# A two-layer graph network on one core: node steps at the end of a pass taken in pairs, one-hot matrices as stationary operands, splits in PSUM, and a preparation that no longer waits for its loads

## The chip, the cores and the metric

One core of a Trainium2 chip runs one launch. The time is device microseconds from start to end of the launch; smaller is better. TensorE is called PE below (its weight loads PEld), VectorE DVE, ScalarE ACT, GpSimd POOL and SyncE SP, as the profile does.

## The reference

A graph of 12,500 nodes with 96 features and 412,500 directed edges, sorted by their target `dst`. Three rounds over all edges have to be computed, each needing the nodes' result of the round before:

```python
e = relu(edge_weight1 @ W_l0 + b_l0) @ W_l1 + b_l1
for layer in (0, 1):                      # two GINE convolutions
    msg = relu(x[src] + e)
    h = x + segment_sum(msg, dst)
    x = relu(relu(h @ Wi0 + bi0) @ Wi1 + bi1)
x = layernorm(x_in + x)
edge_feat = mlp_bn(edge_attr_4)           # linear, relu, batch norm over the edges
m = mlp_bn(concat(x[row], x[col], edge_feat))
x = layernorm(x + segment_sum(m, col) + mlp_bn(x))
```

`mlp_bn` is a linear layer, relu and a normalization with mean and variance over all rows.

## The kernel before

The program is a preparation block (`setup`), three edge passes made by one function `edge_pass` (named `conv0`, `conv1` and `last`), and `finish`. Each is a block of its own: its end is a barrier of all engines.

**An edge pass.** The padded edges are cut into S = 124 slabs of T = 26 tiles of 128 edges. V = 4 slabs make an iteration, so a pass has 31 iterations. A slab is worked on in 7 chunks of four tiles (the last has two). For each tile POOL issues one indirect DMA (`gather`, L254) that fetches the 128 source rows `x[src]` into `got[j]`; there are four such buffers, so POOL can run up to four slabs ahead of the add that consumes them. That is 3,224 gathers in a pass and 9,672 in all. GROUPS cuts the 26 gathers of a slab into two sets with a semaphore each, chunks 0 to 3 and chunks 4 to 6.

For each chunk q a software pipeline (`staged`) runs these steps, each engine in program order: PE `hidden` (L509, the first edge layer), ACT `relu_hidden` (L522), PE `pre` (L1034, the second edge layer in f32, into `ps_pre`), DVE `add_rows` (L598, adds the gathered rows in PSUM), ACT `relu_message` (L543, the message as bf16 part 0), DVE `subtract_first` (L550), ACT `second_part` (L557, bf16 part 1), DVE `third_part` (L563, bf16 part 2), DVE `one_hot` (L1095, for each edge a row of 112 entries with a one at its target's place in the slab's window of 112 nodes), and PE `segment`, whose matmuls `sum_window` (L569) sum the edges by target: for each tile three matmuls, one for each bf16 part, with the 128 x 96 part stationary and the 128 x 112 one-hot moving. At the slab's end DVE `add_window` (L1090) adds the 96 x 112 window from PSUM to `sums`, which holds features by nodes. In `last` there are also squares and sums for the batch norm.

**Node steps.** Once the windows have passed 256 nodes, a node step applies the two node layers (and in `conv1` the layer norm and the products for the last pass), stores its rows to DRAM and lets the next begin. 46 of the 50 steps of `conv0` and of `conv1` are interleaved with the windows; the last four run after the windows, one after the other in a loop (`node_steps`). In `conv0` a step is PE L738, ACT L780, PE L743, ACT L788 twice, PE L748, DVE L822, a store by ACT (L727). In `conv1` it is PE L738, ACT L780, PE L754, DVE L828 to L836, ACT L797, DVE L841 to L847, PE L761, ACT L803, PE L767, ACT L807, PE L774, DVE L855 to L863, and three stores. The next pass gathers from the stored rows, so its first gather comes after the last step's stores, the block's end and a reload of four index tiles by SP (L251).

**Preparation.** `setup` lets POOL issue the gathers of the first two slabs (52) while DVE turns the targets into window positions `rel` and `near_b` and counts whether every edge lies in its window (`fits`). SP issues 25 loads, waits for all 20 constants among them (L323, one of them 4.8 MB of node columns into `sums`), and only then stores `near_b` (L326), waits for it and ends. At the start of `conv0` DVE splits the edge weights `w_f` (128 x 3224 f32, in SBUF) into three bf16 parts (`split`, L273 and L276), which are stored and read back in rows by every slab; it also sets two rows of `sums` (L637, L639). In each of the 31 iterations of `conv0` it splits a piece of the edge attributes in the same way (`split_piece`, L991 and L995, 128 x 416).

## Time and profile before

| | us |
|---|---|
| median of three runs (lowest, highest) | 12338.1 (12335.53, 12362.99) |
| the profiled execution, its own time | 12336.89 |
| its span, first to last instruction | 12335.1 |
| busy: PE, DVE, ACT, POOL | 9812.2, 7390.6, 4942.9, 9165.5 |
| first gather of `conv0`'s block, of `conv1`, of `last` | 94.89, 4116.98, 8223.39 |
| last gather begins | 12252.23 |

The busy times are how long each engine executed something; register, branch and DMA-issuing instructions of the other queues are not in them, but POOL's gathers are. Idle time is put down to what ended it; "issue" is time in which an engine waited for nothing that the profile shows. The rows used here are in the section after the change.

### The profile page before, as it was taken

How to read it: one execution, taken by the hardware profiler on the slowest of the kernel's cores; microseconds unless marked ns; L12 is line 12 of the kernel's file. 1: busy time of each engine (PE TensorE's matmuls, PEld its weight loads, DVE VectorE, ACT ScalarE, POOL GpSimd, SP SyncE). 2: the span in 40 equal slices, each digit the busy share in tenths (PEclk: the TensorE clock that was granted, in tenths of full speed). 3: DMA queues.
4: the chain of work that ended last, by engine and by line, in shares of the span. 5: the costliest groups of instructions: out<-in, count | busy, mean ns of one | idle time of the engine just before them, and what ended most of it. 6: DMA issues, size and time to landing. Idle time of an engine off the chain costs nothing. (4 is left out here: it accounts for less than half of the span.)

```text
span 12335.1 us, 196060 instructions
## 1 busy us (share of the span) xinstructions
PE 9812.2 (80%) x53154; PEld 7907.9 (64%) x53154; DVE 7390.6 (60%) x15235; ACT 4942.9 (40%) x11027; POOL 9165.5 (74%) x9676
## 2 busy tenths in 40 slices
PE   5877777777777788899999999977777777777777
PEld 4766666666666566677777777756666666666666
DVE  5544444444444455566666666657777777777777
ACT  2333333333333344444444444434444444444444
POOL 7777777777777677777777777757777777777775
PEclk9999999999999655555555555555555555555555
DMA  3222222222222222222222222222222222222222
GB/s 92 46 48 47 48 48 47 49 47 47 49 47 47 61 51 50 52 55 56 55 56 54 56 55 56 54 45 52 51 54 52 53 52 53 52 53 52 53 52 53
DMA packets 580897, 647.13 MB, mean 52 GB/s; under 512 B 411337, under 2 KB 411818, under 8 KB 579851
## 3 DMA queue, kind: packets, MB, share of 16 engines
q0 software_dynamic: 309504, 476.02, 18.4%
q1 hardware_dynamic: 216086, 143.43, 5.0%
q10 hardware_dynamic: 54896, 23.80, 0.7%
q14 instruction: 346, 2.83, 0.1%
q8 instruction: 65, 1.06, 0.0%
HBM read 604.68 MB, written 39.43 MB: 52 GB/s over the span
## 5 line engine op out<-in xcount | busy, mean ns | idle before, releaser
L1034 PE MATMUL ps_pre<-w_e,conv_hid 97*128 97x96 f32 x12896 | 3283.8, 435 | 1200.0 <-DVE conv_part L563 1188.3
L1034 PEld LDWEIGHTS ps_pre<-w_e,conv_hid 97*128 97x128 f32 x12896 | 2877.5, 327 | 1925.9 <-issue 1597.7
L1034 PE MATMUL ps_pre<-last_w_q,last_hid 128*128 128x96 f32 x6448 | 1626.0, 432 | 1056.9 <-issue 700.4
L1034 PEld LDWEIGHTS ps_pre<-last_w_q,last_hid 128*128 128x128 f32 x6448 | 1440.2, 327 | 1446.5 <-issue 1022.9
L543 ACT ACTIVATE conv_part<-ps_pre 128x384 bf16<-128x384 f32 x1736 | 815.8, 470 | 3482.4 <-DVE ps_pre L598 3478.0
L569 PE MATMUL ps_win<-conv_hot,conv_part 128*96 128x112 bf16 x19344 | 2164.8, 301 | 0.6 <-DVE conv_part L563 0.6
L569 PEld LDWEIGHTS ps_win<-conv_hot,conv_part 128*96 128x96 bf16 x19344 | 2106.0, 203 | 1.1 <-DVE conv_part L563 0.9
L254 POOL DMA_INDIRECT early_got<-p_rows,early_idx x1612 | 1523.6, 945 | 570.3 <-issue 491.0
L254 POOL DMA_INDIRECT early_got<-h_rows,early_idx x1612 | 1523.0, 945 | 537.5 <-issue 489.1
L254 POOL DMA_INDIRECT early_got<-in_x_rows,early_idx x1612 | 1541.8, 956 | 493.3 <-issue 490.7
L254 POOL DMA_INDIRECT conv_got<-in_x_rows,early_idx x1612 | 1531.3, 950 | 503.6 <-issue 503.3
L254 POOL DMA_INDIRECT last_got<-p_rows,early_idx x1612 | 1523.8, 945 | 491.4 <-issue 491.4
L254 POOL DMA_INDIRECT conv_got<-h_rows,early_idx x1612 | 1521.9, 944 | 491.4 <-issue 490.8
L598 DVE TENSOR_TENSOR ps_pre<-ps_pre,early_got 128x384 f32<-128x384 f32 x1302 | 698.1, 536 | 1685.0 <-PE ps_pre L1034 701.2
L522 ACT ACTIVATE conv_hid<-ps_hid 96x512 f32<-96x512 f32 x1736 | 973.5, 561 | 1027.9 <-PE ps_hid L509 957.3
L598 DVE TENSOR_TENSOR ps_pre<-ps_pre,conv_got 128x384 f32<-128x384 f32 x868 | 464.9, 536 | 1397.2 <-PE ps_pre L1034 576.6
L509 PE MATMUL ps_hid<-conv_row,w_hid 12*96 12x512 bf16 x1736 | 1088.0, 627 | 128.5 <-issue 98.7
L1095 DVE TENSOR_TENSOR conv_hot<-ps_own,rel 128x448 bf16<-128x448 f32 x1736 | 1019.5, 587 | 238.6 <-PE ps_win L569 216.2
L569 PE MATMUL ps_win<-last_hot,last_part 128*97 128x112 bf16 x9672 | 1083.2, 301 | 0.3 <-DVE last_part L563 0.3
L569 PEld LDWEIGHTS ps_win<-last_hot,last_part 128*97 128x97 bf16 x9672 | 1056.7, 207 | 0.6 <-DVE last_part L563 0.4
L563 DVE TENSOR_TENSOR conv_part<-ps_pre,conv_part 128x384 bf16<-128x384 f32 x1736 | 905.4, 522 | 100.7 <-issue 84.2
L557 ACT CAST conv_part<-ps_pre 128x384 bf16<-128x384 f32 x1736 | 786.8, 453 | 414.7 <-DVE ps_pre L550 394.1
(183 smaller groups left out, 10053.1 us busy)
## 6 DMA issues: line engine op xcount, KB each, us to landing
conv_row<-ea_parts SPq DMA_DIRECT2D x372, 84.5 KB
last_row<-ea_parts SPq DMA_DIRECT2D x372, 84.5 KB
early_got<-in_x_rows,early_idx POOLq DMA_INDIRECT x1612, 2.5
conv_got<-in_x_rows,early_idx POOLq DMA_INDIRECT x1612, 2.5
early_got<-h_rows,early_idx POOLq DMA_INDIRECT x1612, 2.5
conv_got<-h_rows,early_idx POOLq DMA_INDIRECT x1612
early_got<-p_rows,early_idx POOLq DMA_INDIRECT x1612
last_got<-p_rows,early_idx POOLq DMA_INDIRECT x1612
```

The source lines that it names most:

```text
L254: gp.indirect_dma_start(to[:, t * C:(t + 1) * C], None, table, bass.IndirectOffsetOnAxis(index[:, t:t + 1], 0)).then_inc(sem, 16)
L509: pe.matmul(ps["hid"][0][0:HC, 0:nt * P], w_hid[:], row[r][AT:AT + K, t0 * P:(t0 + nt) * P], start=True, stop=True).then_inc(s["hid"], 1)
L522: act.activation(hid[b][0:C, 0:nt * P], ps["hid"][0][0:C, 0:nt * P], ACT.Relu).then_inc(s["rhid"], 1)
L543: act.activation(tiles_of(part0[q % NC_], nt, C1), m3, ACT.Relu).then_inc(s["part0"], 1)
L557: act.copy(tiles_of(part1[b], nt, C1), tiles_of(ps["pre"][b], nt, C)).then_inc(s["part1"], 1)
L563: v.tensor_tensor(tiles_of(part2[b], nt, C1), tiles_of(ps["pre"][b], nt, C), tiles_of(part1[b], nt, C1), ALU.subtract).then_inc(s["part2"], 1)
L569: mm = pe.matmul(bank[0:M, 0:width], part[:, t * C1:t * C1 + M], hot_b[:, t * width:(t + 1) * width], start=start and i == 0, stop=stop an ...
L598: v.tensor_tensor(at, at, got[j][:, t0 * C:(t0 + nt) * C], ALU.add).then_inc(s["add"], 1)
L1034: mm = pe.matmul(ps["pre"][q % 2][:, t * C:(t + 1) * C], hid[q % 2][0:P if last else C1, t * P:(t + 1) * P], w_q[j % U][:, c * C:(c + 1) * ...
L1095: v.tensor_tensor(hot[q % 2][:, 0:nt * W].rearrange("p (t w) -> p t w", w=W), iota[:, 0:W].unsqueeze(1).to_broadcast([P, nt, W]), rel[:, b ...
```

## The change

Besides new code for the ends of two passes it consists of six edits.

1. **Pairs at the end.** The four last node steps of `conv0` and `conv1` are no longer a loop. `end_steps` takes 512 nodes at a time (`w` = 0, 1) and writes the stages of both out in turn, with buffers for each in the idle gather buffers and a second PSUM bank. Stores are issued by SP, the last one also without the padding row, whose own store (`none`) is issued first. In `conv1` POOL clears the 1,024 last columns of `sums`.
2. **One-hots as weights.** `sum_tile` makes one matmul for each tile: the one-hot (128 x 112) is stationary, the three parts side by side (128 x 288, or 291 in `last`) move. The window is now 112 nodes by three parts of 96; at the slab's end DVE adds the three (`fold_window`), PE turns the result (`turn_window`), and DVE adds it to `sums` from there. The parts have NB = 4 buffers of all three instead of seven and two and two.
3. **Splits in PSUM.** ACT copies the weights into seven PSUM banks and makes the bf16 parts; DVE subtracts in PSUM. `copy_piece` does the copy for the attributes.
4. **Counts by one operand.** `rel` is shifted by a PSUM operand instead of an SBUF copy of it, and each of the two counts of edges inside is two single-operand comparisons that also sum.
5. **Loads.** The preparation no longer waits for the constants; `conv0` does, before its first matmul. The 4.8 MB of node columns are issued by ACT once the targets have landed. The two rows of `sums` are set at the preparation's end.
6. **Groups.** The gathers of a slab are in three sets: chunks 0 to 3, 4 and 5, and 6.

The core of the diff (the end steps are given as their `conv0` half; that of `conv1` has the same form):

```diff
-GROUPS = [(0, (NC_ + 1) // 2 - 1), ((NC_ + 1) // 2, NC_ - 1)]
+GROUPS = [(0, (NC_ + 1) // 2 - 1), ((NC_ + 1) // 2, NC_ - 2), (NC_ - 1, NC_ - 1)]
...
-                     (gb_msg, a["gb_msg"]), (w_wide, a["w_wide"]), (sums[0:C, :], a["x_cols"]),
+                     (gb_msg, a["gb_msg"]), (w_wide, a["w_wide"]),
...
-                sp.wait_ge(s["const"], 16 * len(loads))
                 sp.wait_ge(s["near"], 32)
...
+                act.wait_ge(s["dst"], 16)
+                act.wait_ge(s["near"], 16)
+                act.dma_start(sums[0:C, :], a["x_cols"]).then_inc(early["cols"], 16)
...
-                go(v.tensor_tensor(rel3, rel3, base_all[:].unsqueeze(2).to_broadcast([P, S, T]), ALU.subtract))
+                go(v.tensor_tensor(rel3, rel3, ps["base"][0][:, 0:S].unsqueeze(2).to_broadcast([P, S, T]), ALU.subtract))
...
-                go(v.tensor_scalar(seen, rel[:], 0.0, None, ALU.is_ge))
-                done()
-                go(v.scalar_tensor_tensor(out=seen, in0=rel[:], scalar=float(W), in1=seen,
-                                          op0=ALU.is_lt, op1=ALU.mult, accum_out=tmp[:, 0:1]))
+                def count(at, x, bound):
+                    go(v.tensor_scalar(inside[0:x.shape[0], 0:x.shape[1]], x, bound, 0.0, ALU.is_ge, ALU.add,
+                                       accum_out=tmp[0:x.shape[0], at:at + 1]))
+                    done()
+                count(10, rel[:], 0.0)
+                count(11, rel[:], float(W))
...
+                count(12, near_f[:], 0.0)
+                count(13, near_f[:], float(R))
...
+                go(v.memset(sums[C:C + 2, :], 1.0))
+                done()
+                go(v.memset(sums[C:C1, :], 0.0))
...
+                def sum_tile(pe, bank, hot_b, q, t, start, stop):
+                    parts = part[q % NB][:].rearrange("p (i x) -> p i x", i=3)[:, :, t * C1:t * C1 + M]
+                    return pe.matmul(bank[0:W, 0:3 * M].rearrange("p (i c) -> p i c", i=3), hot_b[:, t * W:(t + 1) * W], parts,
+                                     start=start, stop=stop)
...
-                        split(go, done, v, w_f[:], [x[:] for x in w_p])
+                        for i in range(2):
+                            for c, (bank, at) in enumerate(cuts):
+                                v.wait_ge(s["wx"], c + 1)
+                                v.wait_ge(s[f"wp{i}"], c + 1)
+                                v.tensor_tensor(bank, bank, w_p[i][:, at], ALU.subtract).then_inc(s[f"wrest{i}"], 1)
...
+                        for w in ENDS:
+                            pe.wait_ge(s["e_z"], w + 1)
+                            pe.matmul(one[w][0:C, :], w_conv[l][1][0:C, :], z_end[w][0:C], start=True, stop=True).then_inc(s["e_b"], 1)
+                        for w in ENDS:
+                            pe.wait_ge(s["e_cols"], w + 1)
+                            for t in range(TW):
+                                mm = pe.transpose(ps["pre"][w][:, t * C:(t + 1) * C], z_end[w][0:C, t * P:(t + 1) * P], ident[0:C, 0:C])
+                            mm.then_inc(s["e_turn"], 1)
...
+                def copy_piece(act, k):
+                    act.wait_ge(s["ef"], 16 * (k + 1))
+                    need(act, s["estep"], k)
+                    act.copy(ps["e"][0][:, 0:D * PIECE], e_f[:]).then_inc(s["ecopy"], 1)
...
+                    def turn_window(k, q):
+                        j, c, _, _ = chunk(q)
+                        if c == NC_ - 1:
+                            pe.wait_ge(s["wsum"], k * V + j + 1)
+                            pe.transpose(turned[j % U][0:M, :], folded[:, 0:M], ident[0:W, 0:W]).then_inc(s["turned"], 1)
...
-                    staged(pe, ITERS, Q, [(0, hidden_rows), (1, pre), (3, segment)],
+                    staged(pe, ITERS, Q, [(0, hidden_rows), (1, pre), (4, turn_window), (3, segment)],
...
+                    def fold_window(k, q):
+                        j, c, _, _ = chunk(q)
+                        if c == NC_ - 1:
+                            bank = ps["win"][j % U]
+                            v.wait_ge(s["seg"], Q * k + q + 1)
+                            need(v, s["turned"], k * V + j)
+                            v.tensor_reduce(folded[:, 0:M], bank[0:W, 0:3 * M].rearrange("p (i c) -> p c i", i=3), AX_X,
+                                            ALU.add).then_inc(s["wsum"], 1)
...
-                    plan += [(1, add_rows)]
+                    plan += [(1, add_rows), (4, add_window)]
...
-                        node_steps(eng, (ITERS - START) * PAIRS, [(s[f"win{r}"], ITERS * PAIRS) for r in range(U)])
+                        end_steps(eng)
```

## Rows read from the trace of the kernel before

**Rows 1.** The page's first part: busy time, share and count of each engine.

```profile
PE 9812.2 (80%) x53154; PEld 7907.9 (64%) x53154; DVE 7390.6 (60%) x15235; ACT 4942.9 (40%) x11027; POOL 9165.5 (74%) x9676
```

**Rows 2.** Groups of POOL: the gathers of the first two passes, by buffer.

```profile
L254 POOL DMA_INDIRECT early_got<-in_x_rows,early_idx x1612 | 1541.8, 956 | 493.3 <-issue 490.7 <-DMA early_idx<-in_src_t 2.3 <-DVE ps_pre L598 0.3
L254 POOL DMA_INDIRECT conv_got<-in_x_rows,early_idx x1612 | 1531.3, 950 | 503.6 <-issue 503.3 <-DVE ps_pre L598 0.3
...
L254 POOL DMA_INDIRECT early_got<-h_rows,early_idx x1612 | 1523.0, 945 | 537.5 <-issue 489.1 <-DMA early_idx<-in_src_t 46.6 <-DVE ps_pre L598 1.8
L254 POOL DMA_INDIRECT conv_got<-h_rows,early_idx x1612 | 1521.9, 944 | 491.4 <-issue 490.8 <-DVE ps_pre L598 0.6
```

**Rows 3.** POOL's timeline: start, duration, instruction, idle time before it.

```profile
18.64 5.13 POOL L254 DMA_INDIRECT early_got<-in_x_rows,early_idx  x1 [0.30 <-issue]
24.08 3.95 POOL L254 DMA_INDIRECT early_got<-in_x_rows,early_idx  x1 [0.30 <-issue]
...
44.12 3.23 POOL L254 DMA_INDIRECT early_got<-in_x_rows,early_idx  x1 [0.30 <-issue]
...
94.89 0.94 POOL L254 DMA_INDIRECT conv_got<-in_x_rows,early_idx  x1 [12.60 <-issue]
...
102.69 4.42 POOL L254 DMA_INDIRECT conv_got<-in_x_rows,early_idx  x1 [0.30 <-issue]
...
4116.98 0.94 POOL L254 DMA_INDIRECT early_got<-h_rows,early_idx  x1 [46.61 <-DMA early_idx<-in_src_t]
...
8223.39 0.94 POOL L254 DMA_INDIRECT early_got<-p_rows,early_idx  x1 [79.27 <-DMA early_idx<-in_src_t]
...
12252.23 0.95 POOL L254 DMA_INDIRECT last_got<-p_rows,early_idx  x1 [0.31 <-issue]
```

**Rows 4.** DVE's timeline in the preparation and at the start of `conv0`.

```profile
18.26 3.52 DVE L371 TENSOR_TENSOR rel<-rel,base_all 128x3224 f32<-128x3224 f32 x1
21.82 1.84 DVE L375 TENSOR_SCALAR inside<-rel 128x3224 f32<-128x3224 f32 x1
23.69 3.52 DVE L377 SCALAR_TENSOR_TENSOR inside<-rel,inside 128x3224 f32<-128x3224 f32 x1
...
42.93 3.61 DVE L388 SCALAR_TENSOR_TENSOR inside<-near_f,inside 124x3328 f32<-124x3328 f32 x1
...
101.60 3.52 DVE L276 TENSOR_TENSOR conv_w_f<-conv_w_f,conv_w_p 128x3224 f32<-128x3224 f32 x1
105.15 1.84 DVE L273 CAST conv_w_p<-conv_w_f 128x3224 bf16<-128x3224 f32 x1
...
115.32 10.72 DVE L637 MEMSET sums<- 2x12800 f32 x1 [2.72 <-issue]
```

**Rows 5.** SP's timeline in the preparation (duration is that of the issue).

```profile
38.30 30.92 SPq L323 DMA_DIRECT2D b_conv<-in_b_conv  x1
...
80.83 0.28 SPq L326 DMA_DIRECT2D near<-near_b  x1
```

**Rows 6.** Windows: length, busy PE, PEld, DVE, ACT, POOL, PEclk, DMA share, GB/s.

```profile
4083.06:4114.45 31.39, 10.74 (x24) 4.02 (x24) 1.43 (x4) 5.20 (x12) 0.00 (x0) 0.53 0.05 14
4089.10:4096.05 6.95, 2.92 (x7) 1.09 (x7) 0.36 (x1) 1.30 (x3) 0.00 (x0) 0.50 0.05 14
...
8165.22:8220.94 55.72, 22.27 (x64) 13.94 (x64) 12.72 (x52) 10.47 (x28) 0.00 (x0) 0.52 0.08 22
8177.23:8190.22 12.99, 5.82 (x17) 3.63 (x17) 3.19 (x13) 2.62 (x7) 0.00 (x0) 0.50 0.08 23
...
5000.00:7000.00 2000.00, 1844.15 (x9294) 1404.53 (x9294) 1227.09 (x2696) 885.46 (x1919) 1512.04 (x1602) 0.50 0.25 55
```

**Rows 7.** Groups by line and shape: sum by target, and reducing a window.

```profile
L569 PE MATMUL ps_win<-conv_hot,conv_part 128*96 128x112 bf16 x19344 | 2164.8, 301 | 0.6 <-DVE conv_part L563 0.6
L569 PEld LDWEIGHTS ps_win<-conv_hot,conv_part 128*96 128x96 bf16 x19344 | 2106.0, 203 | 1.1 <-DVE conv_part L563 0.9
...
L1089 DVE TENSOR_REDUCE slab_sum<-ps_win 96x112 f32 x116 | 30.6, 264 | 17.2 <-issue 17.2
```

More of the change, by code:

```diff
@@ L36 @@
 EARLY = 2
+NB = 4
 Q = V * NC_
@@ L322, in _ @@
                 for to, src in loads:
-                    sp.dma_start(to[:] if not isinstance(to, bass.AP) else to, src).then_inc(s["const"], 16)
-                sp.wait_ge(s["const"], 16 * len(loads))
+                    sp.dma_start(to[:], src).then_inc(early["const"], 16)
+                consts[0] = len(loads)
                 sp.wait_ge(s["near"], 32)
@@ L340, in _ @@
                 pe.wait_ge(s["cnt"], 1)
-                pe.matmul(ps["count"][0][:, 0:2], ones[:], tmp[:, 0:2], start=True, stop=True).then_inc(s["pe"], 1)
+                pe.matmul(ps["count"][0][:, 0:4], ones[:], tmp[:, 10:14], start=True, stop=True).then_inc(s["pe"], 1)
             @block.vector
@@ L467, in edge_pass @@
                                  (pick[1], a["pick1"]), (tail_f, a["tail"])]
-                ps = pools(st, hid=1, pre=2, win=2, own=1, **(dict(feat=1, node=1) if stats else dict(f=1, tot=1) if last else dict(node=1)))
+                ps = pools(st, hid=1, pre=2, win=2, own=1, **(dict(feat=1, node=1) if stats else dict(f=1, tot=1) if last else dict(node=1, e=1)))
+                if split_edges:
+                    pieces = -(-COLS // 512)
+                    wide = -(-COLS // pieces)
+                    cuts = [(x[:, 0:min(wide, COLS - c * wide)], slice(c * wide, min((c + 1) * wide, COLS)))
+                            for c, x in enumerate([*ps["hid"], *ps["pre"], *ps["win"], *ps["node"], *ps["own"]][:pieces])]
+                    assert len(cuts) == pieces and D * PIECE <= 512
                 iota = ps["own"][0][:, CH * C:CH * C + P]
                 squares = ps["own"][0][:, 0:CH * C]
+                turned = [x[:, 512 - W:512] for x in ps["win"]]
                 s = Sems(st, name)
@@ L607, in prepare @@
                 def prepare(v):
[L608 removed]
+                    if not split_edges:
+                        v.tensor_copy(iota, node_row[:])
                     for i in range(2):
                         v.memset(hid[i][64:P, :], 1.0)
[L611 to L614 removed]
+                    for x in part:
+                        v.memset(x[:, 0:CH * C1], 1.0)
+                        v.memset(x[:, CH * C1:3 * CH * C1], 0.0)
                     if stats:
@@ new lines, in gpsimd_end, with end_steps @@
+                def gpsimd_end(gp):
+                    if stats:
+                        gp.wait_ge(s["e_a"], len(ENDS))
+                        gp.memset(sums[0:C, NPAD - END * STEP:NPAD], 0.0).then_inc(s["e_clear"], 1)
+                        gp.wait_ge(s["e_clear"], 1)
+                def end_steps(eng):
+                    if last:
+                        node_steps(eng, (ITERS - START) * PAIRS, [])
+                    else:
+                        {nc.tensor: tensor_end, nc.scalar: scalar_end, nc.vector: vector_end, nc.sync: sync_end,
+                         nc.gpsimd: gpsimd_end}[eng](eng)
@@ L1115, in add_constants @@
                                             ALU.add).then_inc(s[f"qc{r}"], 1)
-                    plan = [(3, lambda k, q: third_part(v, q, q % 2, Q * k + q, left(k, q))),
-                            (4, add_window), (2, one_hot)]
+                    plan = [(3, lambda k, q: third_part(v, q, q % 2, Q * k + q)),
+                            (4, fold_window), (2, one_hot)]
                     if last:
@@ L1275, in both @@
                         node_steps(eng, 0, [(s["slab"], S)])
+                        if stats and eng is nc.sync:
+                            eng.wait_ge(s["step"], STEPS + 1)
+                            eng.dma_start(p_rows[NPAD - 1:NPAD, :], none[:]).then_inc(s["pad"], 16)
+                            eng.wait_ge(s["pad"], 16)
                 @block.sync
```

262 lines of the change are left out of this document (209 added, 53 removed).

## The prediction

> **What bounds the kernel now.** The busy totals come first, and they mislead: PE has 80% of the span, POOL 74%, and no engine looks full [rows 1]. So POOL's groups are read next. One gather lasts 945 ns, and before each POOL sits idle for "issue": 490.8 us over 1,612 gathers is 0.304 us [rows 2]. A gather thus takes a slot of 0.944 + 0.305 = 1.249 us, and during it POOL can begin nothing else. Six groups of 1,612 give 9,672 x 1.249 = 12,080 us of a span of 12,335.1. What POOL waited for in between is almost nothing: 0.3 to 1.8 us for DVE in a group [rows 2]. POOL's chain of gathers is the bound, and everything that PE, DVE and ACT do inside a pass lies beside it.
>
> The other 255 us are then read off POOL's timeline. The first gather starts at 2.7. A gap of 12.6 precedes the gather at 94.89, one of 46.6 the gather at 4116.98, and one of 79.3 the gather at 8223.39 [rows 3]; each contains one ordinary 0.3. The last gather begins at 12252.23, so 12335.1 - 12253.2 = 81.9 us follow it [rows 3]. Together 2.7 + 12.3 + 46.3 + 79.0 + 81.9 = 222. The remaining 33 are gathers longer than normal. Pass 1 against pass 2: 1541.8 - 1523.0 plus 1531.3 - 1521.9 is 28.2 us [rows 2]. Some stand out: 5.13, 3.95, 3.23, 4.42 us [rows 3]. Each lies under long DVE work. The gather at 18.64 ends at 23.77; DVE subtracts from 18.26 to 21.78 and compares from 21.82 to 23.66. The gather at 102.69 ends at 107.11, a subtraction ends at 105.12 and a cast at 106.99 [rows 3, 4]. A gather is held by a DVE operation whose operands are all in SBUF.
>
> The profiled execution took 12336.9, 1.8 more than its span and 1.2 less than the median. I sum differences, so they apply to the median as they are.
>
> **The change, part by part.**
>
> *Counts and shift by one operand (saves about 11 in the preparation, hidden in part).* The gathers at 18.64, 24.08 and 44.12 are 4.19, 3.01 and 2.29 us too long; with two shorter ones beside them, the whole change would remove about 10.8. The casts of the targets stay and so do their stalls, about 4 us. So the 52 early gathers, which end at 82.3 now (94.89 - 12.60 [rows 3]), end near 71.5. The Trainium skill, SBUF — State Buffer, section "Who interferes with whom", says that a two-input DVE operation in SBUF takes only the read side of the port shared with GpSimd, and infers that descriptor generation isn't held by it. The gather at 102.69 disagrees with that inference: it began under the subtraction and could not have lasted 4.42 if only the cast from 105.15 on had held a write at its end of less than 1 us of work [rows 3, 4]. By the inference the subtractions would cost nothing, and some 10 us of what I book here and below would not come: the half-way rival below.
>
> *Where the preparation then ends.* The gap goes only as far as the block's end does. Three things must be over. POOL: 71.5. DVE: its last count now starts later. Targets land as before, near 36.5; then 2.7 of shifts, 1.9 of cast, two counts. The count is not in the trace with a sum: bounds are 1.84 (as L375) and 3.61 (as L388) each [rows 4]. I take 3.6, since the sum makes it more like L388 than L375. That puts DVE near 48.5, some 2 us of small operations 50.5, and then the two rows of `sums`: 2.72 + 10.72 = 13.4 each, both [rows 4], so 77.3. They are moved here from `conv0`'s preparation and cost nothing there any more. SP: the store of `near_b` left at 80.83 because SP sat 30.92 us in the issue of one bias behind the 4.8 MB of columns [rows 5]. Now the columns are in ACT's queue and SP doesn't wait for constants. Best case: the store leaves at 42 and is over long before 77. Worst: small loads and store still share the DMA engines with the columns, and the end stays where it was. I take an end near 80; with the 3 us that lie between a block's end and a first gather, `conv0`'s first gather starts at 83 instead of 94.89: 12 us saved, bounds 0 and 14.6.
>
> *Splits in PSUM (saves 13).* The gathers from 99.9 to 112.5 are 9.2 us too long in all; of them 102.69 alone is 3.5 [rows 3]. DVE's subtractions now have PSUM operands and the casts are ACT's, so I take the 9.2 as gone. For this stands that the add of gathered rows (L598, PSUM with SBUF) runs all through the passes beside gathers of 945 ns [rows 2]. Of the 28.2 of pass 1, 28.2 - 14.9 - 9.2 = 4.1 are the 31 attribute splits; they go too, whose lower bound is 0. ACT's extra work (28 copies of 461, and one of 416 an iteration) delays `conv0`'s first matmuls, but the 26.9 us of memsets are out of the same chain, and POOL is four slabs (130 us) ahead. If that cover were gone, POOL would wait for the first add.
>
> *Pairs at the end of `conv0` (saves 15.5).* From the first matmul of the last steps at 4083.06 to the index reload at 4114.45 are 31.4 us, in which PE works 10.7 [rows 6]. Four steps follow one another at 6.95, of which PE has 2.92 [rows 6]: the rest is handing over, and the store's 2 us of landing that the next step waits for. Written out by pairs, PE's work stands in one row, the other engines mostly beside it: 4 x 2.92 = 11.7 at the slow rate of this stretch, about 9 without what the modelled ends of its matmuls count twice. Behind it come what isn't covered, my estimates from today's steps: a relu 0.6, a copy 0.5, the issue 0.5, landing 2.2. That is 12.8 us instead of the 27 until the last landing now. At the faster rate that PE shows in the first step (2.00 busy against 2.92 [rows 6]) it is 9.5. Saved 14 to 17.6; I take 15.5.
>
> *Pairs at the end of `conv1` (saves 27).* 55.7 us from 8165.22 to 8220.94, PE busy 22.3; a step is 12.99 with 5.82 of PE [rows 6]. In pairs: first layer 3.5, second layer of both 3.4, DVE's residual, statistics and scaling 3.2 for the second pair (as much as all of DVE in a step, 3.19), transposes 1.5, products 6 to 8 for both, DVE's relu and four sums about 4, the last landing 2.3. That is 25 instead of about 51.5; the padding row's own store (2 us after the last step) is no longer behind it. Saved 24 to 31; I take 27.
>
> *One-hots as weights, inside a pass (0).* PE: for each tile 288 columns instead of 3 x 112 = 336. Now they follow each other every 93 ns (78 x 0.093 = 7.3 us a slab); in proportion to columns 26 x 0.24 = 6.2. Added: a transpose, 0.42 (2.92/7 [rows 6]), on DVE a reduction of 288 elements, 0.264 for 112 [rows 7], so 0.45. In pass 2 PE is busy 1844 of 2000 us [rows 6], 30 of the 32.5 us of a slab; with the change 29.4. POOL stays the bound: nothing won or lost. Behind the new wait in PE (`turn_window` for `fold_window`) stand `segment` and the next `hidden`; DVE folds before `one_hot`, while PE is still in `pre`, so the wait should be short.
>
> *At each pass's end (+1.3 in the last).* The last window now goes fold 0.45, transpose 0.5, add 0.27 instead of 0.27: +1 us three times. The shorter sums give about 1 us back over the seven last chunks of `conv0` and `conv1`, where PE sets the pace; in `last` DVE sets it, and it has a second fold there.
>
> *Three groups (0).* Chunks 4 and 5 may start two gathers earlier; the first chunk of the last slab waits for the first set as before and the others follow it at the pace of PE or DVE.
>
> Sum: -12 - 9.2 - 4.1 - 15.5 - 27 + 1.3 = -66.5. 12338.1 - 66.5 = 12271.6.
>
> **The rivals.**
>
> *Half of it.* `near_b`'s store keeps the block open until 91 (0 instead of 12), DVE still holds gathers in the counts, and the pairs give their lower ends (14 and 24): 12338.1 - 9 - 14 - 24 + 2 = 12293. For it speaks the bias's 30.92 us [rows 5]. The Trainium skill, DMA: Bandwidth & Descriptors, section "Issuing engines are not separate DMA queues", says that transfers from all engines' queues end on the same 16 engines and interleave. No row here shows two such queues with these loads; by it another queue for the columns would not shield the store.
>
> *More.* PE runs the tails at its faster rate and the block ends at 77: 12338.1 - 14.6 - 13.3 - 17.6 - 31 + 1.3 = 12263; with shorter chunks in the tails down to 12252.
>
> *PE takes over in pass 2 (slower).* Before, a weight load (203 ns [rows 7]) lay under the matmul before it. If the load of a one-hot shows, by x for each tile, PE's slab is 29.4 + 26x against 32.5 of POOL: it decides from x = 0.12. At the full 0.203 a slab is 34.7: 12338 + 2.2 x 124 - 66 = 12545. Slower than before by 0.3% from x = 0.15. Against it: now the loads hide under 93 ns of matmul, and they'd have 240.
>
> *No change.* The same with x near 0.14, or a `turn_window` that costs each slab of pass 2 some 3.5 us: the tails' gain is eaten, 12300 to 12375.
>
> **How the numbers follow.** 0.62 for the forecast (12260 to 12285), 0.16 for half (to 12300), 0.10 for more, 0.07 for no change, 0.05 for slower. A difference under 0.3%, 37 us, can hardly be told from none. Range 12250 to 12300: it holds the first three. Faster 0.88, same 0.07, slower 0.05.
>
> **What would show it.** Gathers of `conv0` start at 80 to 85 and none before 4060 is above 3 us; gathers' slot stays 1.249 in all passes; the gaps before `conv1` and `last` are about 31 and 53; the end after the last gather is 83. Wrong if the slot grows, if POOL's idle names DVE's add in `conv1`, or if the gather before the first gap is still early and the store of `near_b` late.

## The result, and the profile of the changed kernel

The changed kernel takes 12278.8 us (median of 5 runs, 12276.7 to 12279.5) against 12336.3 for the kernel before in 5 runs on the same chip: ratio 0.9949, 95% interval 0.9937 to 0.9961. That is 57.6 us less; 66.5 were forecast. The profiled execution's span is 12275.7 us.

POOL's timeline is read first, since the gathers were the bound. Its columns are start, duration, the instruction and the idle time before it, here of the changed kernel around the joints of the passes; the rows answer to [rows 3]:

```profile
70.08 0.94 POOL L256 DMA_INDIRECT early_got<-in_x_rows,early_idx  x1 [0.30 <-issue]
96.69 0.94 POOL L256 DMA_INDIRECT conv_got<-in_x_rows,early_idx  x1 [25.66 <-issue]
...
4084.48 0.94 POOL L256 DMA_INDIRECT early_got<-h_rows,early_idx  x1 [28.70 <-DMA early_idx<-in_src_t]
...
8136.64 0.95 POOL L1101 MEMSET sums<- 96x1024 f32 x1 [24.79 <-PE ps_hid L960]
8162.63 0.95 POOL L256 DMA_INDIRECT early_got<-p_rows,early_idx  x1 [25.04 <-DMA early_idx<-in_src_t]
...
12190.67 0.95 POOL L256 DMA_INDIRECT last_got<-p_rows,early_idx  x1 [0.30 <-issue]
```

The 52 early gathers end at 71.0 instead of 82.3, yet `conv0`'s first gather starts at 96.69, no earlier than before (94.89). The joint (POOL's pause between two passes) ahead of `conv1` is 28.7 instead of 46.6 us. The one ahead of `last` is 24.79 + 0.95 + 25.04 = 50.8 instead of 79.3. After the last gather 12275.7 - 12191.6 = 84.1 us remain instead of 81.9.

The groups of gathers come next (total, mean ns, idle before and its releasers); they answer to [rows 2]:

```profile
L256 POOL DMA_INDIRECT early_got<-in_x_rows,early_idx x1612 | 1524.7, 946 | 493.2 <-issue 484.9 <-DVE ps_pre L638 6.1 <-DMA early_idx<-in_src_t 2.2
L256 POOL DMA_INDIRECT conv_got<-in_x_rows,early_idx x1612 | 1520.8, 943 | 516.7 <-issue 516.3 <-DVE ps_pre L638 0.3
L256 POOL DMA_INDIRECT early_got<-h_rows,early_idx x1612 | 1523.0, 945 | 519.7 <-issue 489.8 <-DMA early_idx<-in_src_t 28.7 <-DVE ps_pre L638 1.2
```

Pass 1 has lost 1541.8 - 1524.7 + 1531.3 - 1520.8 = 27.6 us of long gathers; it now has what pass 2 has. The slot stays 0.944 + 0.305. 11.3 us of the 27.6 lie in the preparation, where they are of use only if its end moves; the other 16.4 are on the path (the stretch from `conv0`'s first gather to its last, 3974.5 before, is 3958.1 now).

Why the early end of the gathers bought nothing is seen in the queues of the preparation. ACT's timeline, then SP's, then the end of DVE's:

```profile
41.19 0.41 ACTq L338 DMA_DIRECT2D sums<-in_x_cols  x1
```

```profile
44.35 26.92 SPq L325 DMA_DIRECT2D w_conv<-in_w_conv  x1
71.31 5.03 SPq L325 DMA_DIRECT2D b_conv<-in_b_conv  x1
...
82.76 0.33 SPq L328 DMA_DIRECT2D near<-near_b  x1
94.54 0.35 SPq L1529 DMA_DIRECT2D conv_w_f<-in_w_nat  x1
```

```profile
57.74 10.72 DVE L407 MEMSET sums<- 2x12800 f32 x1 [2.72 <-issue]
71.19 10.72 DVE L409 MEMSET sums<- 1x12800 f32 x1 [2.73 <-issue]
```

ACT issues the 4.8 MB of columns at 41.19. Behind them one of SP's small loads sits 26.92 us in its issue, as 30.92 us of one did before [rows 5], so `near_b`'s store leaves at 82.76, not at 42. The block is over 11.8 us later: SP's first issue of `conv0` is at 94.54. That is the store's own transfer and the block's end behind it: in the four kernels below that keep this preparation the same distance is 11.8 us, and before the change it was 11.9, from the store at 80.83 [rows 5] to

```profile
92.74 0.35 SPq L1283 DMA_DIRECT2D conv_w_f<-in_w_nat  x1
```

DVE ended at 81.91 and didn't matter. Nor did the landing of the early gathers: their queue, q0, moved its last bytes in the stretch 70 to 75 (packets, MB, share of the DMA engines) and nothing from 75 to 94.5:

```profile
q0 software_dynamic: 107, 0.15, 13.1%
```

The start of `conv0` differs from run to run. In the five traces with this same preparation the store left between 79.2 and 86.3, and `conv0`'s first gather began between 93.1 and 100.3. The 94.89 of before lies among them, so the 1.8 us of difference say no more than that nothing was saved.

PE beside [rows 1 and 7], page totals and the group of window sums:

```profile
PE 9503.5 (77%) x34170; PEld 6798.0 (55%) x34170; DVE 7514.9 (61%) x15606; ACT 4947.5 (40%) x11066; POOL 9138.5 (74%) x9677
```

```profile
L603 PE MATMUL ps_win<-conv_part,conv_hot 128*112 128x288 bf16 x6448 | 1906.5, 446 | 0.6 <-DVE conv_part L597 0.5
L603 PEld LDWEIGHTS ps_win<-conv_part,conv_hot 128*112 128x112 bf16 x6448 | 1293.3, 215 | 78.3 <-DVE conv_part L597 2.5
```

19,000 fewer matmuls and 309 us less of busy PE: none of it is in the result. POOL's idle time put down to DVE's add is 19.8 us in the whole run instead of 3.0, but these are 65 of the ordinary pauses of 0.3 us with DVE's name on them, and no longer one is among them.

### The profile page after: what moved, and what is told of

It is laid out like the page before. It is cut to its first block and busy times, and to the rows that moved or that the text cites. A ratio compares the mean times of both kernels' runs of the same rounds, so it can differ in the third digit from the quotient of the medians.

```text
span 12275.7 us, 155459 instructions
## 1 busy us (share of the span) xinstructions
PE 9503.5 (77%) x34170; PEld 6798.0 (55%) x34170; DVE 7514.9 (61%) x15606; ACT 4947.5 (40%) x11066; POOL 9138.5 (74%) x9677
## 5 line engine op out<-in xcount | busy, mean ns | idle before, releaser
L603 PE MATMUL ps_win<-conv_part,conv_hot 128*112 128x288 bf16 x6448 | 1906.5, 446 | 0.6 <-DVE conv_part L597 0.5
L256 POOL DMA_INDIRECT conv_got<-in_x_rows,early_idx x1612 | 1520.8, 943 | 516.7 <-issue 516.3
L256 POOL DMA_INDIRECT early_got<-in_x_rows,early_idx x1612 | 1524.7, 946 | 493.2 <-issue 484.9
L603 PEld LDWEIGHTS ps_win<-conv_part,conv_hot 128*112 128x112 bf16 x6448 | 1293.3, 215 | 78.3 <-DVE conv_part L597 2.5
L603 PE MATMUL ps_win<-last_part,last_hot 128*112 128x291 bf16 x3224 | 964.0, 450 | 0.6 <-DVE last_part L597 0.5
L592 ACT CAST last_part<-ps_pre 128x384 bf16<-128x384 f32 x868 | 397.9, 458 | 1308.4 <-DVE ps_pre L586 1308.4
```

The costliest lines, as they stand in the source:

```text
L256: gp.indirect_dma_start(to[:, t * C:(t + 1) * C], None, table, bass.IndirectOffsetOnAxis(index[:, t:t + 1], 0)).then_inc(sem, 16)
L592: act.copy(part_of(q, 1, nt)[:, :, 0:C], tiles_of(ps["pre"][b], nt, C)).then_inc(s["part1"], 1)
L603: return pe.matmul(bank[0:W, 0:3 * M].rearrange("p (i c) -> p i c", i=3), hot_b[:, t * W:(t + 1) * W], parts, start=start, stop=stop)
```

## The experiments

Unless another base is named, each is the changed kernel with one edit. Times are medians, differences are between them as they stand, also where the two kernels ran on different chips; the kernel before took 12336.3 us beside the changed kernel, 12338.4 in the first group of runs and 12343.0 in the last.

**The pairs undone**, in `both`:

```diff
-                        end_steps(eng)
+                        node_steps(eng, (ITERS - START) * PAIRS, [(s[f"win{r}"], ITERS * PAIRS) for r in range(U)])
```

(and the padding row's store behind the last step again).

> The changed kernel, but the last four node steps of conv0 and conv1 again run one after the other in a loop. If the pairs are what closed the gaps, the gap ahead of conv1's first gather goes from 28.7 us back to about 46 and the one ahead of last's first gather from 50.8 to about 79, and the time rises by 45 to 47 us, to about 12325. Rival: the gaps closed because the sum by target got shorter or the window's end moved; then both gaps stay within 3 us of 28.7 and 50.8 and the time stays near 12279.

Measured 12330.2 us (12322.8 to 12333.6) against 12338.4 before: 0.9993 (0.9983 to 1.0003). POOL's rows at the two joints:

```profile
4103.55 0.94 POOL L256 DMA_INDIRECT early_got<-h_rows,early_idx  x1 [48.78 <-DMA early_idx<-in_src_t]
...
8212.84 0.94 POOL L256 DMA_INDIRECT early_got<-p_rows,early_idx  x1 [80.22 <-DMA early_idx<-in_src_t]
```

48.8 - 28.7 = 20.1 and 80.2 - 50.8 = 29.4: the pairs are worth 49.5 us by the gaps, 51.4 by the medians, and without them the rest of the change is hardly to be told from none. The gap ahead of `conv1` is 2.2 longer than before the change and the one ahead of `last` 0.9, though their steps are the same. The fold and the turn at a pass's end would explain it, but the granted clock differs too (1.00, which is 2.4 GHz, in this kernel's gap ahead of `conv1`, a mean of 0.65 before), so their price is better read where the message parts are stationary again.

**The splits again in SBUF:**

```diff
-                                v.tensor_tensor(bank, bank, w_p[i][:, at], ALU.subtract).then_inc(s[f"wrest{i}"], 1)
+                        split(go, done, v, w_f[:], [x[:] for x in w_p])
...
-                    rest = ps["e"][0][:, 0:n]
+                    rest = e_f[:]
```

> The changed kernel, but weights and attributes are again split by DVE alone with all operands in SBUF. If these operations hold the gathers, three or four gathers just after the start of conv0's block last 2.5 to 5 us again, some 9 us in all, and 31 splits of attributes add about 4: 13 us more, about 12292. Rival: the gathers are held only by DVE's casts, not by its two-operand subtractions; then the long gathers come back with 4 to 6 us in all and the time is about 12285.

Measured 12291.4 us (12290.3 to 12296.0), 0.9963 (0.9949 to 0.9977): 12.6 slower than the changed kernel; the stretch of `conv0`'s gathers is 3972.3 instead of 3958.1, 14.2 more, and its preparation happened to end 1.7 earlier. POOL, then DVE, in the same microseconds:

```profile
99.97 2.05 POOL L256 DMA_INDIRECT conv_got<-in_x_rows,early_idx  x1 [0.30 <-issue]
102.33 5.12 POOL L256 DMA_INDIRECT conv_got<-in_x_rows,early_idx  x1 [0.30 <-issue]
107.75 5.12 POOL L256 DMA_INDIRECT conv_got<-in_x_rows,early_idx  x1 [0.30 <-issue]
```

```profile
100.06 1.84 DVE L275 CAST conv_w_p<-conv_w_f 128x3224 bf16<-128x3224 f32 x1 [2.65 <-DMA conv_w_f<-in_w_nat]
101.94 3.52 DVE L278 TENSOR_TENSOR conv_w_f<-conv_w_f,conv_w_p 128x3224 f32<-128x3224 f32 x1
105.49 1.84 DVE L275 CAST conv_w_p<-conv_w_f 128x3224 bf16<-128x3224 f32 x1
107.36 3.52 DVE L278 TENSOR_TENSOR conv_w_f<-conv_w_f,conv_w_p 128x3224 f32<-128x3224 f32 x1
110.92 1.84 DVE L275 CAST conv_w_p<-conv_w_f 128x3224 bf16<-128x3224 f32 x1
```

The gather that starts at 102.33 ends at 107.45, 0.12 after the cast behind the subtraction; the next ends 0.11 after the next cast. A gather that begins under a subtraction with two SBUF operands lasts through it and through the cast that follows.

**The message parts stationary again** (three matmuls of 112 columns a tile, no fold, no turn):

```diff
-                            mm = sum_tile(pe, ps["win"][r], hot[q % 2], q, t, t0 + t == 0, t0 + t == T - 1)
+                            for i in range(3):
+                                mm = pe.matmul(ps["win"][r][0:M, 0:W], part_of(q, i, CH)[:, t, 0:M], hot[q % 2][:, t * W:(t + 1) * W],
+                                               start=t0 + t == 0 and i == 0, stop=t0 + t == T - 1 and i == 2)
```

> The changed kernel, but the sums by target are again three matmuls for each tile with the parts stationary, and the window goes to sums straight from PSUM. My theory: inside the passes POOL sets the time, so nothing changes there; each pass's end loses the fold and the turn (about 1 us each) and gains them back in longer sums: 12277 to 12280. Rival: one-hots as weights relieve PE in conv1, where it is busy over nine tenths; then conv1 is longer by more than 5 us here and POOL's waits for DVE's add grow.

Measured 12274.9 us (12271.9 to 12278.2), 0.9947 (0.9931 to 0.9964). The stretches 4200 to 8100 of both kernels (PE, PEld, DVE, ACT, POOL busy, granted clock, DMA share, GB/s), first the changed one, then this one:

```profile
4200.00:8100.00 3900.00, 3453.37 (x11886) 2370.43 (x11886) 2413.92 (x5270) 1700.26 (x3680) 2948.52 (x3123) 0.50 0.25 54
```

```profile
4200.00:8100.00 3900.00, 3551.22 (x17996) 2708.03 (x17996) 2377.95 (x5150) 1709.94 (x3680) 2948.97 (x3121) 0.50 0.23 54
```

98 us more of busy PE in `conv1`, and POOL has the same 2949 us of gathers. So the one-hots as weights move nothing inside a pass. At the ends my expectation was wrong: the median lies below the 12277 to 12280 that I gave, and the longer sums take nothing back. The gap ahead of `conv1` is 25.9 instead of 28.7 and the end after the last gather 82.0 instead of 84.1; the gap ahead of `last` is 50.6 against 50.8. The profiled execution shows it less, since its `conv0` began at 100.25:

```profile
100.25 0.94 POOL L256 DMA_INDIRECT conv_got<-in_x_rows,early_idx  x1 [29.19 <-issue]
```

**The columns issued only when the store has landed:**

```diff
-                act.wait_ge(s["near"], 16)
+                act.wait_ge(s["nearout"], 16)
                 act.dma_start(sums[0:C, :], a["x_cols"]).then_inc(early["cols"], 16)
```

> The changed kernel, but ACT issues the 4.8 MB of node columns only when the store of near_b has landed. In the changed kernel that store leaves at 82.8 us and conv0's first gather starts at 96.7. Theory A: the columns' transfer, though in another queue, shares the DMA engines with SP's constants and keeps SP in their issue; without it the store leaves near 50, DVE's two memsets end the block at about 82, the first gather is at about 85 and the time falls by 12 us to 12267. Theory B: the constants' many small pieces ahead of the store in SP's own queue are what delays it; then the store still leaves after 70 and the time falls by less than 8 us.

Measured 12280.2 us (12272.3 to 12280.5), 0.9951 (0.9934 to 0.9967): nothing gained. ACT's and SP's rows:

```profile
67.37 0.38 ACTq L337 DMA_DIRECT2D sums<-in_x_cols  x1
```

```profile
55.15 0.33 SPq L328 DMA_DIRECT2D near<-near_b  x1
...
96.48 0.35 SPq L1528 DMA_DIRECT2D conv_w_f<-in_w_nat  x1
```

The store did leave at 55.15, 27.6 us sooner, and had landed by 67.37; DVE ended at 81.8; the block ended at 96.5 all the same. So the time part of my theory fell. What was late next is in the transfers. First the stretch 70 to 90; q10 carries ACT's columns, q0 the gathers:

```profile
q10 hardware_dynamic: 80, 4.10, 96.9%
q0 software_dynamic: 64, 0.10, 2.6%
```

Then q0 in the stretch 90 to 93, behind which it moves nothing up to 98:

```profile
q0 software_dynamic: 32, 0.05, 9.2%
```

POOL had issued its last early gather by 70.9. The 0.15 MB of early gathers that were left at 70 took until 92.9, while the columns moved; in the changed kernel, whose columns were over by then, 0.15 MB were moved before 75. POOL's next gather is 27.68 us behind its last. So this edit made a new holder: with the columns moved to 67 and later, they are on the way when the last gathers have to land. The columns end at 92.9 too, so this run can't tell whether the block waited for the gathers' landing or for theirs. The next kernels take the columns out of the block.

**The columns in `conv0`'s block:**

```diff
-                act.dma_start(sums[0:C, :], a["x_cols"]).then_inc(early["cols"], 16)
...
                         act.wait_ge(s["wf"], 16)
+                        act.dma_start(sums[0:C, :], a["x_cols"]).then_inc(s["cols"], 16)
```

> The changed kernel with one move: ScalarE issues the load of the node columns inside conv0's block, once the weights' input has landed, instead of in the preparation. Nothing else changes. Theory A (the preparation's end is held by two things, the offset store behind the shared transfers and the landing of the 52 early gathers behind the columns' large packets; with the columns out of the preparation neither holds): the store leaves at about 55 us as in the run where the columns waited for it, the early gathers' last bytes land by about 75, the block ends when VectorE's two clearings of the sums do, at about 82, and the first gather of conv0 starts at 84 to 86 instead of 96.7: 12278.8 - 12 = 12267 us (12263 to 12271). Theory B (the block's end is set by something else that comes 12 to 15 us after the last work, such as the engines' barrier or the loading of conv0's instructions): the first gather starts at 95 to 99 again, 12279 us. Theory C (the columns are only moved: their 25 us of transfers starve conv0's first gathers, and the first window sums wait for the columns): the first gather starts at 85, but the early slabs land late and GpSimd waits for it in the first 300 us, 12275 us or more.

**The same, and the rows of ones set in `conv0` again:**

```diff
-                go(v.memset(sums[C:C + 2, :], 1.0))
-                done()
-                go(v.memset(sums[C:C1, :], 0.0))
...
                         go(v.memset(w_hid1[:], 0.0))
+                        go(v.memset(sums[C:C + 2, :], 1.0))
+                        done()
+                        go(v.memset(sums[C:C1, :], 0.0))
```

> As the last kernel (columns loaded inside conv0's block), and the two clearings of the sums' rows (10.7 us each with 2.7 us ahead of each) go back from the preparation to VectorE's work at conv0's start, where they stood before the change. Theory A (the block then ends with the latest of GpSimd's 52 gathers, which are issued by 71 and land by about 75, and the store, which lands by about 67): first gather of conv0 at 77 to 79, 8 us ahead of the kernel with the columns moved alone: 12259 us (12255 to 12264). VectorE has 27 us more to do at conv0's start, which is hidden as in the kernel before, where it stood there too, as long as GpSimd's first wait for a free slab comes later than the first sums. Theory B (that work delays the first sums, and GpSimd waits for the first slab's buffer by what is gained): 12267 us, with a wait of GpSimd of 5 to 10 us in the first 300 us.

**That, with the shift and the counts by two SBUF operands again:**

```diff
-                count(10, rel[:], 0.0)
-                count(11, rel[:], float(W))
+                go(v.tensor_scalar(seen, rel[:], 0.0, None, ALU.is_ge))
+                done()
+                go(v.scalar_tensor_tensor(out=seen, in0=rel[:], scalar=float(W), in1=seen,
+                                          op0=ALU.is_lt, op1=ALU.mult, accum_out=tmp[:, 0:1]))
```

> As the kernel with the columns and the rows moved, and VectorE's counts and the shift of the destinations again as before the change: the shift reads the bases from SBUF beside the destinations, and each count is a comparison and then a multiply of two SBUF operands with the sum. Theory A (an operation of VectorE with two large operands in SBUF holds the start of a gather that falls in it by its length, and this was worth 11 us ahead of the end of the 52 early gathers): the last early gather ends at about 82 us instead of 71, the first gather of conv0 starts 10 to 11 us later than without this edit (at about 88), 12269 us. Theory B (the counts' form was worth nothing, and the early gathers come sooner after the change because the constants' loads are spread over two queues): the last early gather ends at 71 to 73 again, no difference to the kernel without this edit.

**The columns, the rows and the parts stationary together:**

> As the kernel with the columns and the rows moved, and the window sums again with the message parts as the stationary operand (three matmuls of 112 columns a tile and no fold and turn at the end of a slab) as before the change. Theory A (in a pass TensorE's time is hidden either way, and the fold and turn of the last slab stand uncovered at the end of each pass, 1 to 3 us three times): 2 to 6 us less than the kernel without this edit, 12255 us if that one has 12259. Theory B (the one-hots as weights give VectorE or TensorE room that shows somewhere in a pass): as much or more than without this edit, with waits of GpSimd in conv1 or the last pass.

These four ran on another chip, on which the kernel before itself takes 18160 us (18145 to 18170); they took 19095, 19095, 19087 and 19493 us. Up to `conv0`'s first gather nothing differs, so the preparation can be read there; their whole times tell nothing of it. First gather of `conv0` with the columns moved, then with the rows too, then with the old counts:

```profile
83.78 0.94 POOL L256 DMA_INDIRECT conv_got<-in_x_rows,early_idx  x1 [12.11 <-issue]
```

```profile
78.18 0.94 POOL L256 DMA_INDIRECT conv_got<-in_x_rows,early_idx  x1 [7.20 <-issue]
```

```profile
18.42 5.13 POOL L256 DMA_INDIRECT early_got<-in_x_rows,early_idx  x1 [0.30 <-issue]
23.86 3.95 POOL L256 DMA_INDIRECT early_got<-in_x_rows,early_idx  x1 [0.30 <-issue]
...
89.61 0.94 POOL L256 DMA_INDIRECT conv_got<-in_x_rows,early_idx  x1 [7.20 <-issue]
```

With the columns gone the store leaves at 55.1 and `conv0` starts when DVE's memsets are over (80.6): 83.78, where I had forecast 83. With the rows gone too, POOL itself is the last: 7.20 us behind its last gather. Its queue moved the last 0.10 MB in the stretch 70 to 73, and nothing from 73 to 77.8:

```profile
q0 software_dynamic: 64, 0.10, 14.1%
```

The old counts bring back the gathers of 5.13 and 3.95 us [rows 3], the last early gather ends at 82.4 instead of 71.0, and the 7.20 stay, so the start moves by the whole 11.4. The form of the shift and the counts is worth that once nothing else holds the block.

What the other chip slows is outside the preparation. PE in `conv0` there, of the kernel with columns and rows moved:

```profile
2018.74 2.00 PE L1256 MATMUL ps_pre<-w_e,conv_hid 97*128 97x96 f32 x8 [6.80 <-issue]
...
2035.31 0.66 PE L534 MATMUL ps_hid<-conv_row,w_hid 12*96 12x512 bf16 x1 [13.62 <-issue]
```

The instructions shown last as long as elsewhere, but PE, DVE and ACT each stand some 5 to 16 us once or twice a slab, with no instruction or transfer of this stretch named as what ended it (the rows say only issue or remote), and POOL waits for the adds. These variants are 5% slower there than the kernel before, and the one with the parts stationary 7%. The changed kernel itself wasn't run there, and no trace of the kernel before was taken there; the cause stays open, and so does whether the change gains anything on such a chip.

**Two of them on a third chip**, where the kernel before takes 12343.0 us (12337.2 to 12355.2).

> The same kernel as the one with the columns loaded in conv0's block and the rows of ones cleared there, run again because on the chip of its first run the kernel before itself took 18160 us, and every engine stood 5 to 14 us a slab with nothing to wait for in its rows. The first run showed the preparation as theory A has it: the early gathers end at 71.0, conv0's first gather starts at 78.2 instead of 96.7. Theory A (on a chip where the kernel before takes 12336 us, those 18.5 us go through to the end): 12278.8 - 18.5 = 12260 us (12256 to 12265), and no wait of GpSimd in the first 300 us. Theory B (the work moved into conv0 delays the first sums and GpSimd waits for the first slab's buffer): 12267 us or more, with such a wait in the rows of the first 300 us.

Measured 12262.1 us (12261.2 to 12265.1), 0.9936 (0.9922 to 0.9949). First gather of `conv0` at 78.38; in the first 300 us POOL waits once, 1.12 us. The 18.3 us of earlier start are 16.7 us of the end by the two medians, which are of different chips.

> As the kernel with the columns and the rows moved, and the message parts stationary again in the window sums (three matmuls a tile, no fold and turn), on a chip where the kernel before takes 12336 us. Theory A (TensorE's time inside a pass is hidden either way, and the fold and turn of the last slab stand uncovered at each pass's end, 1 to 3 us three times): 2 to 7 us less than the kernel without this edit, 12255 us if that one has 12260; the gap ahead of conv1 25.9 instead of 28.7, ahead of the last pass 50.6 instead of 49.8 to 51.4, 82.0 after the last gather instead of 84.1. Theory B (it is the same or slower, within 2 us): the one-hots as weights cost nothing at the ends. On the other kind of chip, where the engines stand without a reason in the rows, this edit made the kernel 400 us slower (19493 against 19095), since there TensorE's own time is on the path.

Measured 12257.1 us (12256.1 to 12274.4; four of five within 1.2), 0.9931 (0.9918 to 0.9945): 5.0 less than without the edit. Its gap ahead of `conv1` is 25.4 against 28.5, ahead of `last` 51.3 against 53.2, the end after the last gather 82.2 against 84.2: 7.0 in sum, in the profiled execution, which is the one of 12274.4 us: its three stretches from first to last gather are 18.0 us longer in sum than those of the kernel without the edit, at 1.8 to 2.0 ns more for each slot. The 1.9 ahead of `last` also go with a mean granted clock of 0.57 instead of 0.50.

The expectation gives TensorE's own time as the reason for the 400 us on the other chip. The traces from there don't bear it out: the edit lengthens the stretch of gathers by 130 us in `conv0` and 280 in `last`, and in `conv1`, where TensorE is busiest, by nothing (6368.0 against 6370.2).

**Two groups of gathers instead of three:**

```diff
-GROUPS = [(0, (NC_ + 1) // 2 - 1), ((NC_ + 1) // 2, NC_ - 2), (NC_ - 1, NC_ - 1)]
+GROUPS = [(0, (NC_ + 1) // 2 - 1), ((NC_ + 1) // 2, NC_ - 1)]
```

> The changed kernel with a slab's gathers again in two groups (chunks 0 to 3, and 4 to 6) instead of three (0 to 3, 4 and 5, 6), nothing else. Theory A (a group is only the unit in which VectorE waits for landed rows; the last group's last gather decides the slab's end in both, so that inside a pass nothing changes): 12278 us, within 2 us of the changed kernel. Theory B (with the third group chunks 4 and 5 are summed 2.5 us before the last two gathers land, which shortens each pass's end by the work of two chunks, 3 to 5 us three times, since only chunk 6 stands behind the last gather): 12288 to 12292 us, with the gaps ahead of conv1 and of the last pass and the stretch after the last gather each 3 to 5 us longer (28.7, 51 and 84.1 before).

Measured 12279.6 us (12274.1 to 12283.6), 0.9950 (0.9937 to 0.9964); gaps 28.7 and 49.6, end 83.9. No difference: theory A. Its `conv0` began at

```profile
93.13 0.94 POOL L256 DMA_INDIRECT conv_got<-in_x_rows,early_idx  x1 [22.05 <-issue]
```

## Why the prediction was right, and the step of it that was not

**The bound** was read rightly: the slot of a gather stayed 1.249 us in all passes, and PE's work, changed by 98 us in one pass either way, moved nothing.

**The preparation, -12 forecast, +1.8 measured** (94.89 to 96.69, with 93.1 to 100.3 in the five traces of this preparation, so about nothing). This is the term that was mis-sized. Some of its parts held: gathers over at 71.0 (71.5 forecast), DVE at 81.9 (77.3; the targets landed later, at 41, and the counts took the 3.6 us I had taken). What failed is the sentence "Best case: the store leaves at 42 and is over long before 77" as the case I built on. It left at 82.76, since the columns, from ACT's queue, held SP's issues as they had from SP's own. The Trainium skill, DMA: Bandwidth & Descriptors, section "Issuing engines are not separate DMA queues", speaks for this side, and the trace agrees: 26.92 us in one small load's issue. My rival "half of it" had this step right, at 0, but was wrong on the counts and the pairs. In the changed kernel the store was the only holder, since the gathers had landed 20 us before. A second one, which I hadn't seen, appeared when the columns were only put off to 67: then the gathers' last bytes and the columns both ended at 92.9 and kept the block open to 96.5. With the columns out of the block the forecast's 83 comes out as 83.8. Part of that is luck: by my own sum DVE was over at 77.3, and I took an end near 80 with no step that gave it.

**Splits, -13.3 forecast, -16.4 measured** over `conv0`'s stretch, 12.6 to 14.2 by undoing them; the 2.2 between are not attributed. Every long gather beside the subtractions is gone. The 9.2 at the start were sized rightly. The attributes' 4.1 were too low: beside the three long ones, 50 gathers of `conv0` were longer than 0.96 us before, by 6.8 us in sum, and one is now. The prediction's sentence "A gather is held by a DVE operation whose operands are all in SBUF" was too wide: the counts with a running sum (3.51 us) and the memsets of `sums` (10.72 us) leave the gathers beside them at 0.94. The inference in the Trainium skill, SBUF — State Buffer, section "Who interferes with whom", that an operation with two inputs in SBUF doesn't hold descriptor generation, disagrees with the traces: 5.12 us beside a subtraction of 3.52 and the cast behind it against 0.94 alone. The same section of the Trainium skill also says that a DVE instruction with two SBUF inputs contends with a GpSimd instruction that reads SBUF; these gathers read their indices from there, so with that sentence the traces agree.

**Pairs, -15.5 and -27 forecast.** The gaps shrank by 17.9 and 28.5, in which the fold and the turn are already paid; by undoing them alone the pairs are worth 20.1 and 29.4. I had the steps right. Ahead of `conv1` the sum was 4.6 us low. Three stretches show what the clock has in it (length, busy PE, PEld, DVE, ACT, POOL, granted clock, DMA share, GB/s): the pairs ahead of `conv1`, the loop there in the kernel with the pairs undone, and the gap ahead of `last` in the kernel with the columns and the rows moved.

```profile
4068.20:4078.00 9.80, 7.44 (x17) 2.67 (x17) 1.38 (x3) 3.88 (x6) 0.00 (x0) 0.97 0.08 20
```

```profile
4054.80:4103.50 48.70, 23.20 (x67) 12.25 (x65) 11.81 (x28) 9.76 (x22) 0.00 (x0) 1.00 0.06 11
```

```profile
8095.57:8148.78 53.21, 34.09 (x121) 26.55 (x120) 26.03 (x81) 13.01 (x29) 0.95 (x1) 0.50 0.13 31
```

The pairs ran at 0.97, nearly all of it the upper level, where the four steps before had 0.53 [rows 6]; that is the faster rate that I had kept for the rival "more". It doesn't make the gain, since the loop at 1.00 still took 48.7 us. Ahead of `last` the 29.4 set a loop at 0.50 against pairs at a mean of 0.57; against the pairs at 0.50 they are 80.2 - 53.2 = 27.0, as forecast.

**One-hots as weights, 0 inside a pass: right. At the passes' ends** I had +1 three times with 2 us given back. Measured: +2.2 after the last gather, and by undoing it in two kernels 2.0 to 2.1 there and 2.8 to 3.2 ahead of `conv1`. Ahead of `last` the undoing gives 0.2 and 1.9, and the four traces with fold, turn and a granted clock of 0.57 spread from 49.6 to 51.4, so nothing can be read. Nothing is given back at the other two.

In sum, by the gaps: +1.8 - 16.4 - 17.9 - 28.5 + 2.2 = -58.8, and pass 2's and 3's gathers are within a microsecond. The span is 59.4 shorter, the median 57.6. From the 66.5 forecast 13.8 us are missing in the preparation and 0.9 at the last end; the splits gave 3.1 and the joints 3.9 more than booked. So two errors in opposite directions, 14.7 and 7.0 us, partly cancel in the time; that the total came near is in part luck.

The best version found is the changed kernel with the columns and the rows of ones moved into `conv0` and the parts stationary: 12257.1 us, 22 less than the changed kernel, and also 22 less than the one with two groups, which ran on the same chip. Its ratio's interval still meets the changed kernel's; its `conv0` begins at 78.0, outside the 93.1 to 100.3 of the other preparation. On the chip where the kernel before takes 18160 us it is the slowest of all.

## What to carry to other kernels

Before booking an earlier block end, list everything that the block waits for, the landing of each engine's own last transfers included, and ask for each what large transfer is on the way at that time; here one load of 4.8 MB held first a store, and when it was put off by 26 us, the end of the block itself. Issuing a large load from another engine didn't free the queue behind it: it has to be moved in time, to where nothing waits. Before reading a microsecond or two as an effect, see how far kernels with the same code in that stretch differ: here 7 us at the first gather of `conv0`, and 0.2 at the gap ahead of `conv1`. And a saving of busy time on an engine that isn't the bound was worth nothing, while what it needs at the end of a pass (a fold, a turn) was paid.

## What the runs showed of the chip that I hadn't expected

- While the 4.8 MB of columns moved (12,800 floats a row), the last 0.15 MB of GpSimd's queue took from 70 to 92.9; without columns on the way the last 0.10 MB took less than 3 us. A small load's issue on SP lasted 26.92 us behind them, and 0.50 us where they were put off.
- Where nothing else held the block, the next one's first gather came 7.20 us behind the last early gather in five executions, with the gathers' last bytes moved 6.0 to 6.1 us ahead of it. With late columns it came 27.68 us behind the last gather and 5.8 behind the last bytes. That a block waits for the landing of GpSimd's gathers fits both, but no run takes the landing away alone, and the late columns ended at the same time, so it is argued and not shown.
- A comparison with one SBUF operand and a running sum takes 3.51 us for 3,224 elements a partition, as long as one with two, where the plain one takes 1.84; but it leaves the gathers at 0.94.
- The granted clock in the profile reads 1.00 (2.4 GHz) from 1000 to 3500, in `conv0`, and 0.50 (1.2 GHz) from 5000 to 7500, in `conv1`; the window sums' matmuls of 288 columns last 447 ns in the median in both.
- On one chip the kernel before took 18160 us instead of 12336 and two of the variants 19095 and 19493 instead of 12262 and 12257, with 50% of busy PE instead of 78 and 80%, and the same totals of busy time within 1%.
